# Four store places and five load places in the layer norm of a sparse graph layer

## The chip, the cores and the metric

The kernel runs on one core of a Trainium2 chip. The metric is device time in microseconds (us), the median of several executions. PE is TensorE, DVE is VectorE, ACT is ScalarE, POOL is GpSimd and SP is SyncE, whose queue issues most DMAs. A core's DMAs run on 16 DMA engines.

## The reference

```python
# x: (8192, 512) float32; adj: (8192, 8192) float32, some 0.1% of it above zero, a diagonal among it
h = maximum(layernorm(x), 0)
mask = adj > 0
head = mask / maximum(sqrt(sum(mask * mask, axis=-1)), 1e-12)
inc = adj + head
out = x + (inc @ h) / sum(inc, axis=-1)
```

The layer norm has no weights, and its eps is 1e-5. adj has 256 MB and is read once. x, h and out have 16 MB each.

## The kernel before

**The layer norm (LN).** The 8192 rows are taken in LN = 16 chunks of 512 rows; each of the 128 partitions holds ROWS = 4 rows of 512 values, 8 KB. A chunk is loaded by SP (ln_load, L340), 1 MiB in one DMA. DVE computes its statistics (ln_chunk, L703 to L712), with a root by ACT in between (ln_sqrt, L513). ACT writes relu of the normalised rows into a store place (ln_apply, L520), four instructions, and raises ln_done. SP stores the place to h_scratch in HBM (ln_store, L344), 1 MiB again. h_scratch is what the gathers read later.

**The places.** The first HELD_CHUNKS = 5 chunks are loaded into x_held, where they stay for the residual. The other eleven go round through XBUFS = 3 places of four slots in gathered_rows (G, 22 slots of 512 values). The store places are slots 12 to 19 of the same buffer, two places, taken in turn (hst). ln_apply of chunk c waits on h_stored[c % 2], so for the store of chunk c-2. ln_load of chunk c, from c = 8 on, waits until ln_done is c - XBUFS + 1, so for chunk c-3.

**SP's order.** SP first issues ln_load of chunks 0 to 3. Then for c = 4 to 15 it issues ln_store(c-4), which waits for ln_done of that chunk, and ln_load(c). Then comes chunk 0 of adj's tile 0, and then the last four stores, with adj chunks 1 to 3 of tile 0 between them (load_chunk, L352); then the four chunks of tile 1 with no wait, and from tile 2 on the loads of the scan, each of which waits until DVE and ACT have read the chunk it overwrites (L349, L351).

**The scan.** adj is taken in 64 tiles of 128 rows. adj_tile (A, 128 partitions x 2 x 8192 values) holds two tiles, A[:, t % 2]. A tile is loaded in four chunks of 1 MiB, each 1024 columns of the left and of the right half. For each chunk DVE folds the two halves into one (fold, L720), finds the eight largest words (L742) and their places (L746). ACT counts zeros over the chunks (check, L533). The small operations of the tiles before are placed between these, by an order written out by hand (period). POOL gathers the rows of h that a tile needs by indirect DMA (L454), 8 own slots and 3 spill slots a tile, into gathered_rows. PE sums them with diagonal and spill matrices (L1157, L1165), and brings the spilled entries of a tile together (L1130), for which DVE waits at L863. POOL waits for all of h_stored before its first gather. DVE starts on tile 0 when its part of the layer norm is over.

At the start POOL clears slots 20 and 21 of gathered_rows (L430), which no place of the layer norm uses.

Of the kernel before, what the change touches and what calls it, by code (L numbers as in the profile page):

```python
# [7 lines left out]
def add_graph_layer(nc, x, adj, out):  # L8
# [4 lines left out]
    ACT = mybir.ActivationFunctionType  # L13
    AX = mybir.AxisListType

    N, D = x.shape
# [31 lines left out]
    ROWS = 4  # L48
    LN = N // (P * ROWS)
# [2 lines left out]

    HELD_CHUNKS = 5
    HELD = ROWS * HELD_CHUNKS
    XBUFS = 3

    KB = N // P
    HCH = 8
# [10 lines left out]
    with ctx:  # L69
        def sb(name, shape, dt):  # L70
            return ctx.enter_context(nc.sbuf_tensor(name, shape, dt))

        def sem(name):
            return ctx.enter_context(nc.semaphore(name))

        h = nc.dram_tensor("h_scratch", [N, D], fp32, kind="Internal").ap()
        h_ln = h.rearrange("(c p j) d -> c p j d", p=P, j=ROWS)
        h_blk = h.rearrange("(c k p) d -> c p k d", p=P, k=HCH)

        A = sb("adj_tile", [P, 2, N], fp32)  # L80
        F = sb("folded", [P, 2, CW], fp32)
        G = sb("gathered_rows", [P, 2 * (OWN + EXTRA), D], fp32)
# [91 lines left out]
        def xin(c):  # L174
            if c < HELD_CHUNKS:
                return held[:, ROWS * c:ROWS * (c + 1), :]
            b = (c - HELD_CHUNKS) % XBUFS
            return G[:, ROWS * b:ROWS * (b + 1), :]

        def hst(b):  # L180
            return G[:, ROWS * (XBUFS + b):ROWS * (XBUFS + 1 + b), :]

        def x_of(t):
            return held[:, t] if t < HELD else xres[:, t % 2]
# [10 lines left out]
        def chunk(b, j):  # L195
            return A[:, b, 2 * CW * j:2 * CW * (j + 1)].rearrange("p (h c) -> p h c", h=2)
# [5 lines left out]
        def diag_chunk(t):  # L202
            return t // ROWS * P * ROWS % HALF // CW
# [48 lines left out]
        ln_rstd = sem("ln_rstd")  # L252
        ln_scaled = sem("ln_scaled")
        ln_done = sem("ln_done")
        h_stored = [sem(f"h_stored{b}") for b in range(2)]
        adj_loaded = [[sem(f"adj_loaded{b}{j}") for j in range(CHUNKS)] for b in range(2)]
        x_loaded = [sem(f"x_loaded{b}") for b in range(2)]
        checked = sem("checked")
# [76 lines left out]
        @block.sync  # L335
        def _(sp):
            def ln_load(c):
                if c >= HELD_CHUNKS + XBUFS:
                    sp.wait_ge(ln_done, c - XBUFS + 1)
                sp.dma_start(xin(c), x_ln[c]).then_inc(ln_loaded[c % 8], 16)  # L340

            def ln_store(c):
                sp.wait_ge(ln_done, c + 1)
                sp.dma_start(h_ln[c], hst(c % 2)).then_inc(h_stored[c % 2], 16)  # L344

            def load_chunk(t, j):
                if t >= 2:
                    sp.wait_ge(folded, CHUNKS * (t - 2) + j + 1)
                    sp.wait_ge(checked, 4 * (t - 2) + 2 * (j // 2) + 2)  # L349
                    if j == diag_chunk(t - 2):  # L350
                        sp.wait_ge(diag_read, t - 1)  # L351
                sp.dma_start(chunk(t % 2, j), adj_h[t // ROWS, t % ROWS, :, :, CW * j:CW * (j + 1)]).then_inc(adj_loaded[t % 2][j], 16)  # L352

            def load_x(t):
                if t >= HELD + 2:
                    sp.wait_ge(own_done, t - 1)
                sp.dma_start(xres[:, t % 2], x_t[t // ROWS, t % ROWS]).then_inc(x_loaded[t % 2], 16)

            def store_tile(t):
                sp.wait_ge(out_ready, t + 1)  # L360
                sp.dma_start(out_t[t // ROWS, t % ROWS], osb[:, t % 2]).then_inc(out_stored[t % 2], 16)

            for c in range(4):
                ln_load(c)
            for c in range(4, LN):
                ln_store(c - 4)
                ln_load(c)
            load_chunk(0, 0)
            for c in range(LN - 4, LN):
                ln_store(c)  # L370
                if c < LN - 1:
                    load_chunk(0, c - (LN - 4) + 1)
            for j in range(CHUNKS):
                load_chunk(1, j)
            for t in range(TILES):
                if t + 2 < TILES:
                    load_chunk(t + 2, 0)
                    load_chunk(t + 2, 1)
                if t >= 4:
                    store_tile(t - 4)  # L380
                if t >= HELD:
                    load_x(t)
                if t + 2 < TILES:
                    load_chunk(t + 2, 2)
                    load_chunk(t + 2, 3)
            for t in range(TILES - 4, TILES):
                store_tile(t)
            for b in range(2):
                sp.wait_ge(out_stored[b], 16 * (TILES // 2))

            sp.wait_ge(list_ready, 1)
            n = sp.value_load(badnu[0:1, 0:1], min_val=0, max_val=TILES)
            with sp.If(n > 0):
                with sp.Fori(0, n) as j:
                    row = sp.value_load(badu[0:1, bass.ds(j, 1)], min_val=0, max_val=FIRST_ROW)
                    sp.wait_ge(batch_stored, 16)
                    sp.dma_start(A[:, 0, :], adj[bass.ds(row, P, step=ROWS), :]).then_inc(d_adj, 16)
                    sp.dma_start(xres[:, 0], x[bass.ds(row, P, step=ROWS), :]).then_inc(d_x, 16)
                    for c in range(NCH):
                        if c >= 2:  # L400
                            sp.wait_ge(d_mm, j * KB + (c - 1) * HCH)
                        sp.dma_start(G[:, HCH * (c % 2):HCH * (c % 2 + 1), :], h_blk[c]).then_inc(d_h[c % 2], 16)
                    sp.wait_ge(d_out, j + 1)
                    sp.dma_start(out[bass.ds(row, P, step=ROWS), :], osb[:, 0]).then_inc(d_stored, 16)
                    sp.wait_ge(d_stored, j * 16 + 16)
                    sp.sem_inc(passed, 1)

        @block.gpsimd
        def _(pool):
            steps = [0]  # L410

            def step(ins):
                steps[0] += 1
                ins.then_inc(const_step, 1)
                pool.wait_ge(const_step, steps[0])
# [11 lines left out]
            step(nc.gpsimd.memset(cap[:], 3.0e38))  # L427
            on_diagonal(cap[:], 0, 0.0)
            step(nc.gpsimd.memset(on_diag[:, BATCH:BATCH + 1], 0.0))
            step(nc.gpsimd.memset(G[:, ROWS * (XBUFS + 2):], 0.0))  # L430
            step(nc.gpsimd.memset(ones[:], 1.0))
            step(nc.gpsimd.memset(zero_unit[:], ZERO))
            step(nc.gpsimd.memset(count_eps[:], 1e-24))
# [25 lines left out]
            def gather_own(t):  # L459
                b = t % 2  # L460
                pool.wait_ge(idx_ready, t + 1)
                if t >= 2:
                    pool.wait_ge(own_done, t - 1)
                for s in range(OWN):
                    gather(slot(b, s), idx[:, b, s:s + 1], own_gathered[b][s // CHUNKS])
# [6 lines left out]
                for g in range(EXTRA):  # L472
                    gather(slot(b, OWN + g), spidx[:, b, g:g + 1], spill_gathered[b])

            for b in range(2):
                pool.wait_ge(h_stored[b], 16 * (LN // 2))
            gather_own(0)
            gather_own(1)
            for t in range(2, TILES):
# [30 lines left out]
        def _(act):  # L510
# [3 lines left out]

            def ln_apply(c):
                act.wait_ge(ln_scaled, c + 1)
                if c >= 2:
                    act.wait_ge(h_stored[c % 2], 16 * (c // 2))
                for j in range(ROWS):
                    last = nc.scalar.activation(hst(c % 2)[:, j], xin(c)[:, j], ACT.Relu,  # L520
                                                bias=nb[:, c, j:j + 1], scale=rs[:, c, j:j + 1])
                last.then_inc(ln_done, 1)

# [114 lines left out]
            for c in range(LN):  # L638
                ln_sqrt(c)
                ln_apply(c)  # L640
# [634 lines left out]
```

## Time and profile before

| what | us |
|---|---|
| median of 3 runs | 1341.62 |
| lowest and highest of them | 1336.1, 1348.91 |
| the profiled execution, its own time | 1334.34 |
| span of the profiled execution (first to last instruction) | 1332.6 |

The profile is of one execution. Times in it count from the start of the span. An instruction's busy time is that of its engine; a DMA issue on SP is short, and its transfer runs on the DMA engines afterwards. The DMA share is the mean busy share of the 16 DMA engines, and GB/s is what they moved; a share near 1 with few GB/s means packets that took long.

### The profile page before, as it was taken

The page shows a single profiled execution, that of the slowest core. Times are in us where ns is not written, and L with a number is a line of the kernel's source. Part 1 is how long each engine was busy: PE and PEld are TensorE (multiplying, and loading weights), DVE is VectorE, ACT ScalarE, POOL GpSimd, SP SyncE. Part 2 cuts the span into 40 slices and gives each one's busy share as a digit, 9 for nine tenths or more (in the row PEclk, how much of TensorE's full clock was granted, in tenths as well). Part 3 has the DMA queues.
Part 4 walks back from the last instruction along what each step waited for, and adds up shares of the span by engine and source line. Part 5 has one row for each costly group of instructions (what it writes and reads, how often), then busy time and mean ns, then how long its engine had stood idle before and what let it go on. Part 6 is the DMA issues. An engine that isn't in the chain of part 4 may idle for free.

```text
span 1332.6 us, 14627 instructions
## 1 busy us (share of the span) xinstructions
PE 940.4 (71%) x2670; PEld 457.0 (34%) x2670; DVE 1168.8 (88%) x2845; ACT 978.6 (73%) x1905; POOL 777.0 (58%) x746
## 2 busy tenths in 40 slices
PE   0000887867887887787887888887788878788634
PEld 0000343333443443333443333443343433343312
DVE  5549999889989999898999899999799899898253
ACT  5447886878887887887888787778788788787321
POOL 1002567556676667576667675666666666677413
PEclk9999999899998999998899988989999989999677
DMA  8999999999999999999999999999999999996321
GB/s 346 336 353 406 396 375 376 340 377 356 380 390 345 377 393 388 377 388 373 385 392 389 372 391 375 390 377 376 383 397 391 388 388 388 383 382 227 108 84 42
DMA packets 147390, 469.14 MB, mean 352 GB/s; under 512 B 24752, under 2 KB 24752, under 8 KB 143149
## 3 DMA queue, kind: packets, MB, share of 16 engines
q1 hardware_dynamic: 89792, 330.33, 64.5%
q0 software_dynamic: 57504, 137.85, 28.7%
q8 instruction: 24, 0.39, 0.1%
q14 instruction: 70, 0.57, 0.1%
HBM read 488.64 MB, written 33.82 MB: 392 GB/s over the span
## 4 chain that ended last, share of the span: by engine, by line
DVE 63%; issue 18%; DMA 6%; another core or an unknown queue 5%; ACT 5%; POOL 1%; PE 1%; DVEq 0%; SPq 0%; ACTq 0%; POOLq 0%
DVE cand_word L742 21%; DVE folded L720 21%; DVE cand_index L746 8%; DMA h_scratch<-gathered_rows 5%; ACT gathered_rows L520 2%; ACT junk L533 1%; DVE diagonal_alone L727 1%; DVE entry L878 1%; DVE folded L736 1%; DVE weights_and_payload L841 1%; DMA adj_tile<-in_adj_dram,bad_row_number 1%; DVE entry_sign L784 1%; DVE inc L829 1%; ACT diag L592 1%
## 5 line engine op out<-in xcount | busy, mean ns | idle before, releaser
L454 POOL DMA_INDIRECT gathered_rows<-h_scratch,slot_column x520 | 559.6, 1076 | 310.9 <-issue 159.0
L1157 PE MATMUL acc<-gathered_rows,diag 128*128 128x512 f32 x1040 | 494.6, 620 | 90.3 <-DMA gathered_rows<-h_scratch,slot_column 74.7
L533 ACT ACTIVATE junk<-adj_tile,zero_unit 128x2048 bf16<-128x2048 f32 x256 | 509.9, 2000 | 4.9 <-DMA adj_tile<-in_adj_dram 4.9
L454 POOL DMA_INDIRECT gathered_rows<-h_scratch,spill_column x195 | 208.5, 1069 | 227.3 <-ACT spill_column L575 163.5
L1157 PEld LDWEIGHTS acc<-gathered_rows,diag 128*128 128x128 f32 x1040 | 197.3, 197 | 339.0 <-issue 338.8
L742 DVE MAX8 cand_word<-folded 128x8 f32<-128x1024 f32 x256 | 312.8, 1222 | 0.5 <-issue 0.3
L746 DVE FIND_INDEX8 cand_index<-cand_word,folded 128x8 uint32<-128x1024 f32 x256 | 312.2, 1219 | 0.0
L720 DVE SCALAR_TENSOR_TENSOR folded<-adj_tile 128x1024 f32<-128x1024 f32 x256 | 310.9, 1215 | 0.0
L1165 PE MATMUL acc<-gathered_rows,spill_matrix 128*128 128x512 f32 x390 | 220.6, 711 | 90.8 <-DMA gathered_rows<-h_scratch,spill_column 74.1
L592 ACT ACTIVATE diag<-ident,weights_and_payload 128x128 f32<-128x128 f32 x584 | 177.3, 387 | 32.7 <-issue 17.6
L1165 PEld LDWEIGHTS acc<-gathered_rows,spill_matrix 128*128 128x128 f32 x390 | 81.7, 223 | 181.2 <-issue 181.2
L609 ACT ACTIVATE out_tile<-acc 128x512 f32<-128x512 f32 x65 | 38.5, 593 | 133.4 <-remote 63.7
L1112 PE MATMUL poff<-spill_rank,lanes_before 128*128 128x1 f32 x128 | 18.2, 212 | 120.0 <-DVE spill_rank L791 119.8
L1151 PE MATMUL acc<-own_row,diag 128*128 128x512 f32 x128 | 71.7, 644 | 42.9 <-ACT own_row L602 26.3
L1112 PEld LDWEIGHTS poff<-spill_rank,lanes_before 128*128 128x128 f32 x128 | 24.3, 192 | 150.5 <-issue 149.0
L863 DVE TENSOR_TENSOR own_entry<-pbrought,place_plus_half 128x72 f32<-128x72 f32 (+1 forms) x65 | 14.8, 228 | 65.1 <-remote 58.5
L1130 PEld LDWEIGHTS pbrought<-weights_and_payload,owner 128*128 128x128 f32 x390 | 54.8, 195 | 36.8 <-issue 36.8
L520 ACT ACTIVATE gathered_rows<-gathered_rows,ln_bias,ln_rstd 128x512 f32<-128x512 f32 x44 | 32.2, 802 | 36.7 <-DMA h_scratch<-gathered_rows 36.7
L1136 PE MATMUL pturned<-ident,owner 128*128 128x128 f32 x390 | 58.4, 287 | 0.0
L1130 PE MATMUL pbrought<-weights_and_payload,owner 128*128 128x72 f32 (+1 forms) x390 | 53.2, 274 | 5.1 <-issue 3.7
L583 ACT ACTIVATE spill_matrix<-pturned,entry 128x128 f32<-128x128 f32 x195 | 56.8, 366 | 0.0
L1151 PEld LDWEIGHTS acc<-own_row,diag 128*128 128x128 f32 x128 | 23.7, 199 | 80.3 <-issue 55.4
(152 smaller groups left out, 860.2 us busy)
## 6 DMA issues: line engine op xcount, KB each, us to landing
adj_tile<-in_adj_dram SPq DMA_DIRECT2D x256, 1024.0 KB
h_scratch<-gathered_rows SPq DMA_DIRECT2D x16, 1024.0 KB, 8.9
out_dram<-out_tile SPq DMA_DIRECT2D x64, 256.0 KB
gathered_rows<-in_x_dram SPq DMA_DIRECT2D x11, 1024.0 KB, 7.3
x_residual<-in_x_dram SPq DMA_DIRECT2D x44, 256.0 KB
gathered_rows<-h_scratch,slot_column POOLq DMA_INDIRECT x520
x_held<-in_x_dram SPq DMA_DIRECT2D x5, 1024.0 KB, 8.1
gathered_rows<-h_scratch,spill_column POOLq DMA_INDIRECT x195
```

Source lines behind the costliest of these rows:

```text
L454: nc.gpsimd.indirect_dma_start(out=into, out_offset=None, in_=h[:, :], in_offset=bass.IndirectOffsetOnAxis(ap=column, axis=0), bounds_chec ...
L520: last = nc.scalar.activation(hst(c % 2)[:, j], xin(c)[:, j], ACT.Relu, bias=nb[:, c, j:j + 1], scale=rs[:, c, j:j + 1])
L533: nc.scalar.activation(junk[:, n % 2].rearrange("p (j c) -> p j c", j=2), both[:, :, half], ACT.Relu, bias=zero_unit[:], scale=-UP, accum_ ...
L592: last = nc.scalar.activation(diag[:, t % 2, s], ident[:], ACT.Copy, scale=wpay[:, t % 2, s:s + 1])
L720: nc.vector.scalar_tensor_tensor(out=F[:, j % 2], in0=a[:, 1], scalar=UP, in1=a[:, 0], op0=ALU.mult, op1=ALU.add).then_inc(folded, 1)
L742: nc.vector.max(out=cv[:, t % 2, 8 * j:8 * j + 8], in_=F[:, j % 2]).then_inc(vals_found, 1)
L746: nc.vector.max_index(out=ci[:, t % 2, 8 * j:8 * j + 8], in_max=cv[:, t % 2, 8 * j:8 * j + 8], in_values=F[:, j % 2]).then_inc(idx_found, 1)
L1130: last = nc.tensor.matmul(pbrought[:, 3 * n * g:3 * n * (g + 1)], owner[:, g * P:(g + 1) * P], wpay[:, t % 2, 1 + OWN:1 + OWN + 3 * n], st ...
L1136: last = nc.tensor.matmul(pturned[:, g * P:(g + 1) * P], owner[:, g * P:(g + 1) * P], ident[:], start=True, stop=True)
L1151: nc.tensor.matmul(acc[t % 3][:], diag[:, t % 2, 0], again[:], start=False, stop=False)
L1157: last = nc.tensor.matmul(acc[t % 3][:], diag[:, t % 2, 1 + s], slot(t % 2, s), start=False, stop=False)
L1165: last = nc.tensor.matmul(acc[t % 3][:], W[:, t % 2, g], slot(t % 2, OWN + g), start=False, stop=(g == EXTRA - 1))
```

## The change

XBUFS goes from 3 to 5, so loaded chunks from the sixth on go round through five places, slots 0 to 19 of gathered_rows. The store places leave gathered_rows: there are four, in the half of adj_tile that holds tile 1 (A[:, 1]), a quarter of it each. h_stored has four semaphores instead of two. Because the stores read what tile 1's loads overwrite, SP now waits for all stores before it issues the first chunk of tile 1.

```diff
-    XBUFS = 3
+    XBUFS = 5
...
         def hst(b):
-            return G[:, ROWS * (XBUFS + b):ROWS * (XBUFS + 1 + b), :]
+            return A[:, 1, ROWS * D * b:ROWS * D * (b + 1)].rearrange("p (j d) -> p j d", j=ROWS)
...
-        h_stored = [sem(f"h_stored{b}") for b in range(2)]
+        h_stored = [sem(f"h_stored{b}") for b in range(4)]
...
             def ln_store(c):
                 sp.wait_ge(ln_done, c + 1)
-                sp.dma_start(h_ln[c], hst(c % 2)).then_inc(h_stored[c % 2], 16)
+                sp.dma_start(h_ln[c], hst(c % 4)).then_inc(h_stored[c % 4], 16)
...
                 if c < LN - 1:
                     load_chunk(0, c - (LN - 4) + 1)
+            for b in range(4):
+                sp.wait_ge(h_stored[b], 16 * (LN // 4))
             for j in range(CHUNKS):
                 load_chunk(1, j)
...
-            step(nc.gpsimd.memset(G[:, ROWS * (XBUFS + 2):], 0.0))
+            step(nc.gpsimd.memset(G[:, ROWS * XBUFS:], 0.0))
...
-            for b in range(2):
-                pool.wait_ge(h_stored[b], 16 * (LN // 2))
+            for b in range(4):
+                pool.wait_ge(h_stored[b], 16 * (LN // 4))
...
             def ln_apply(c):
                 act.wait_ge(ln_scaled, c + 1)
-                if c >= 2:
-                    act.wait_ge(h_stored[c % 2], 16 * (c // 2))
+                if c >= 4:
+                    act.wait_ge(h_stored[c % 4], 16 * (c // 4))
                 for j in range(ROWS):
-                    last = nc.scalar.activation(hst(c % 2)[:, j], xin(c)[:, j], ACT.Relu,
+                    last = nc.scalar.activation(hst(c % 4)[:, j], xin(c)[:, j], ACT.Relu,
                                                 bias=nb[:, c, j:j + 1], scale=rs[:, c, j:j + 1])
```

## Rows read from the trace of the kernel before

**Rows 1.** The page: busy time by engine, and two of its costliest groups.
```profile
PE 940.4 (71%) x2670; PEld 457.0 (34%) x2670; DVE 1168.8 (88%) x2845; ACT 978.6 (73%) x1905; POOL 777.0 (58%) x746
...
L1157 PE MATMUL acc<-gathered_rows,diag 128*128 128x512 f32 x1040 | 494.6, 620 | 90.3 <-DMA gathered_rows<-h_scratch,slot_column 74.7
...
L720 DVE SCALAR_TENSOR_TENSOR folded<-adj_tile 128x1024 f32<-128x1024 f32 x256 | 310.9, 1215 | 0.0
```

**Rows 2.** Table of stretches: from:to, us; engines' busy time (count); PE clock, DMA share, GB/s.
```profile
0.00:38.00 38.00, 0.00 (x0) 0.00 (x0) 22.07 (x75) 21.09 (x34) 5.87 (x28) 1.00 0.89 354
...
21.00:38.00 17.00, 0.00 (x0) 0.00 (x0) 9.62 (x33) 9.45 (x17) 0.00 (x0) 1.00 1.00 420
38.00:43.00 5.00, 0.00 (x0) 0.00 (x0) 3.18 (x11) 3.09 (x7) 0.00 (x0) 1.00 0.92 220
43.00:51.00 8.00, 0.00 (x0) 0.00 (x0) 3.65 (x14) 3.07 (x6) 0.00 (x0) 1.00 0.96 402
...
76.00:82.00 6.00, 0.00 (x0) 0.00 (x0) 3.38 (x12) 3.02 (x5) 0.00 (x0) 1.00 0.81 255
82.00:90.00 8.00, 0.00 (x0) 0.00 (x0) 3.89 (x13) 3.02 (x5) 0.00 (x0) 1.00 0.97 338
...
38.00:98.10 60.10, 0.00 (x0) 0.00 (x0) 29.36 (x101) 27.32 (x47) 0.00 (x0) 1.00 0.93 337
98.10:113.70 15.60, 0.00 (x0) 0.00 (x0) 15.26 (x21) 10.98 (x12) 0.00 (x0) 1.00 1.02 406
...
0.00:113.67 113.67, 0.00 (x0) 0.00 (x0) 66.65 (x195) 59.39 (x91) 5.87 (x28) 1.00 0.93 352
```

**Rows 3.** Waits from 0 to 130 us: us in total, times, longest.
```profile
ACT gathered_rows L520 <- DMA h_scratch<-gathered_rows: 43.2, 14, 6.8
...
DVE ln_stats L703 <- DMA gathered_rows<-in_x_dram: 6.1, 5, 1.7
```

**Rows 4.** The tile h_scratch from 0 to 125 us: issue to landing of its DMAs.
```profile
DMA to landing us min/median/max: 4.8/8.9/12.3
```

**Rows 5.** Timeline of the first 20 us: start, duration, engine, line, operation.
```profile
0.80 2.04 SPq L340 DMA_DIRECT2D x_held<-in_x_dram  x4
...
5.72 2.47 DVE L703 BATCH_NORM_STATS2 ln_stats<-x_held 128x6 f32<-128x512 f32 x4 [5.72 <-DMA x_held<-in_x_dram]
...
14.00 2.48 DVE L703 BATCH_NORM_STATS2 ln_stats<-x_held 128x6 f32<-128x512 f32 x4
...
17.51 2.47 DVE L703 BATCH_NORM_STATS2 ln_stats<-x_held 128x6 f32<-128x512 f32 x4
```

**Rows 6.** Timeline around 38 us: chunk 8's load, chunk 5's store, chunk 8's statistics.
```profile
38.05 0.33 SPq L340 DMA_DIRECT2D gathered_rows<-in_x_dram  x1
...
38.43 0.43 SPq L344 DMA_DIRECT2D h_scratch<-gathered_rows  x1
...
45.02 2.47 DVE L703 BATCH_NORM_STATS2 ln_stats<-gathered_rows 128x6 f32<-128x512 f32 x4 [1.56 <-DMA gathered_rows<-in_x_dram]
```

**Rows 7.** Timeline of the hand-over from the layer norm to the scan.
```profile
94.74 2.93 ACT L520 ACTIVATE gathered_rows<-gathered_rows,ln_bias,ln_rstd 128x512 f32<-128x512 f32 x4 [6.75 <-DMA h_scratch<-gathered_rows]
...
98.12 1.23 DVE L720 SCALAR_TENSOR_TENSOR folded<-adj_tile 128x1024 f32<-128x1024 f32 x1
...
102.66 0.33 SPq L344 DMA_DIRECT2D h_scratch<-gathered_rows  x1
103.03 58.43 SPq L352 DMA_DIRECT2D adj_tile<-in_adj_dram  x20
...
113.67 1.21 DVE L720 SCALAR_TENSOR_TENSOR folded<-adj_tile 128x1024 f32<-128x1024 f32 x1
```

**Rows 8.** Two later stretches, and DVE's longest waits from 98 to 1270 us.
```profile
100.00:165.00 65.00, 28.26 (x76) 13.95 (x77) 64.58 (x135) 50.38 (x82) 26.49 (x25) 0.97 1.02 401
...
230.00:295.00 65.00, 49.69 (x148) 24.46 (x146) 55.64 (x133) 49.95 (x100) 38.96 (x39) 0.94 0.97 364
...
DVE own_entry L863 <- remote: 58.5, 15, 7.8
```

## The prediction, made before the change was run

> **What bounds the kernel now.** The page comes first. VectorE (DVE) is busy 88% of the span, more than any other engine, its fold of a chunk (L720) had no idle time before it in 256 executions, and PE's product with gathered rows (L1157) waited 74.7 us for gathers [rows 1]. That is a mean over stages. The change touches only the layer norm (about 0 to 103 us) and the hand-over to the scan of adj, so I read those by themselves.
>
> The table of stretches shows two kinds of time in the layer norm [rows 2]. From 21 to 38 us the DMA engines move 420 GB/s at a share of 1.00. After that slow and fast stretches alternate: 220 GB/s in 38 to 43 us, 402 in 43 to 51, and so on to 255 in 76 to 82 (four slow stretches, at 38, 51, 63 and 76 us). From 38 to 98.1 us the mean is 337 GB/s, while DVE works 29.4 us of 60.1 and ScalarE (ACT) 27.3.
>
> The waits say who is late: ACT's layer-norm pass (L520) waited 43.2 us in 14 waits for a store to h_scratch to land, DVE only 6.1 us in 5 for a load [rows 3]. A store takes 8.9 us in the median from issue to landing, 12.3 at most [rows 4]. So the loop is: chunk c is normalised, its store is issued, it lands 8.9 us later, and only then may chunk c+2 be written into the same place, which takes 2.93 us plus 0.5 us of root, reciprocal and bias. (8.9 + 3.4) / 2 = 6.2 us a chunk. The trace has the L520 pass over chunk 14 begin at 94.74, after 6.75 us of waiting [rows 7]. The work itself could go faster: DVE's statistics of chunks 2 and 3 start 3.51 us apart (14.00 and 17.51) [rows 5].
>
> **The change, part by part.** *Four store places instead of two.* Chunk c now waits for the store of chunk c-4: (8.9 + 3.4) / 4 = 3.1 us a chunk, less than the 3.5 us of the compute chain. Even a store of 12.3 us [rows 4] gives only 3.9. This wait ceases to decide. What is late next is the transfer itself: each chunk is a 1 MiB load and a 1 MiB store, 2.10 MB, or 5.2 us at 406 GB/s and 5.0 us at 420. The layer norm becomes bound by DMA bandwidth.
>
> *Five load places instead of three.* The load of c now waits for chunk c-5, but SP issues the store of c-4 just ahead of it, which waits for chunk c-4. So SP runs four chunks ahead, not five; before it was three. Four chunks ahead is 4 x 5.2 = 20.7 us from one load to the time its chunk must be done, less about 6.6 us from landing to normalised; 14 us of transfers stay queued, over 5 MB. The queue does not run dry. Before, load and store issued at 38.05 and 38.43 met a nearly empty queue and the load was only read at 45.02, 7 us on [rows 6].
>
> *What rate.* This is the largest unknown. Upper end: 420 GB/s, loads and stores mixed with a queue that held several transfers (21 to 38 us). Lower end: 337, the mean of 38 to 98.1 us, if the slow stretches belong to the mixture and not to the nearly empty queue. For the empty queue: the first slow stretch follows one, and the fast stretch behind it has the next pair of transfers issued on top. Against: 82 to 90 us ran at 338 GB/s [rows 2], with the last load of x, two chunks of adj and stores queued, by SP's order. I take 406, the rate of 98.1 to 113.7 us, in which a full queue of adj loads and the last stores runs.
>
> *The sum to the hand-over.* The first 38 us stay as they are: 354 x 38 = 13.45 MB moved, and the last 17 of them at full rate already. Only the four first loads are issued up front, as before. In SP's order the last store is the 36th transfer of 1.049 MB (16 loads, 16 stores, 4 chunks of tile 0), so 37.75 MB. At 406 GB/s its last byte goes at 38 + (37.75 - 13.45) / 0.406 = 97.9 us (95.9 at 420, 110.1 at 337).
>
> *The new wait of SP.* Before, tile 1's first chunk was issued at 103.03, right behind the last store at 102.66 [rows 7]. Now SP waits until all 16 stores have landed, since the four places lie in tile 1's buffer. Behind that wait stands everything that SP issues from tile 1 on, first the four loads of tile 1; DVE's fold of chunk (1,0) and ACT's check of (1,0) and (1,1) wait for them. I add about 0.8 us until the last store is confirmed (an estimate between 0 and 2.3 us: the shortest store took 4.8 us [rows 4], of which 1.05 MB at 420 GB/s are 2.5, and the rest lies at both its ends), and 4.9 us for a load into an empty queue, from the issue at 0.80 to DVE's start at 5.72 [rows 5]. Chunk (1,0) is folded at 97.9 + 5.7 = 103.6 us instead of 113.67 [rows 7]: 10.1 us earlier (12.1 at 420, 2.1 later at 337). The chunks behind it come every 2.6 us, and DVE needs 3.7 to 3.9, so the gap is paid once.
>
> *Tile 0.* Load 15 is transfer 28: 77.2 us, with about 1 us to land; DVE's last layer-norm operations end some 3.4 us later, so the first fold comes near 82 instead of 98.12 us. Sixteen us, but they are not kept: the rest of tile 0's chunks alternate with stores, 5.2 us apart, so DVE waits between folds, and chunk (0,3) comes at 38 + (36.7 - 13.45) / 0.406 + 1 = 96.3 us. Its 3.7 us of work end before the 103.6 of chunk (1,0). No engine's work grows: the same 64 passes of L520, 16 loads and 16 stores. POOL waits on four semaphores for one moment, long before its first gather needs anything. SP's semaphore waits cost nothing where they are already met.
>
> *What the rest keeps.* From 100 to 165 us DVE is busy 64.58 of 65 us and DMA has a share of 1.02; from 230 to 295 DVE has 55.64 of 65 [rows 8]. Its largest wait is L863, 58.5 us in 15 waits, for what PE brings over. PE in turn waits for gathers [rows 1], which share the DMA engines. If DVE's position sets the rest, all 10.1 us stay. If DMA's position does, less: after the change 38.8 MB (36 transfers and one chunk) are moved by 103.6 us, before by 38.8 / 0.352 = 110.2 us [rows 2], 6.6 us. For the first tiles DVE is nearer the bound, over the whole run both; I take 8.5 us.
>
> In the profiled execution (1334.34 us, span 1332.6) that makes 1325.8. It lies 7.3 us under the median of the three runs; on the median, 1341.6 - 8.5 = 1333.1 us.
>
> **The rivals.**
> *A: the mixture of loads and stores is what is slow; the new wait then decides.* Place: SP's wait for all stores. At 337 GB/s the last store's byte goes at 110.1 us, chunk (1,0) is folded at 115.8, 2.1 us late, and 38.8 MB are moved then instead of at 110.2, 5.6 us late. Price: 2 to 6 us slower, 1346 us in the middle. It decides below 24.3 / (113.67 - 5.7 - 38) = 347 GB/s. For it: 338 GB/s in 82 to 90 us, with transfers queued, and the DMA share of 0.93 over the whole slow part. Against: 420 GB/s for 17 us on the same mixture.
>
> *B: a ceiling between the two.* A rate near 358 GB/s would put the last byte at 105.9 and the fold at 111.6, 2 us gained by DVE and 1.4 us lost by the DMA position (111.6 against 110.2): 1341 us, no change. The rows speak against it as a ceiling with 420, 402 and 406 GB/s. The Trainium skill, "DMA: Bandwidth & Descriptors", section "Where 436 GB/s comes from", says that for transfers between HBM and SBUF the HBM side, about 358 GB/s for a core, binds. By that rule this change would bring nothing. The trace does not agree: its own rows reach 420 GB/s.
>
> *C: the hand-over is early, and the gain is given back.* The rest of the run waits on gathers and PE in a loop of its own, and starts with 3 to 4 adj chunks less loaded ahead than before. If that lead carried the first tiles, stalls at L863 come sooner: a gain of 0 to 4 us, 1340 us. For it: DMA shares of 0.97 to 1.03 to the end. Against: DVE never waited for an adj load [rows 1].
>
> *D: more than forecast.* 420 GB/s or more (12.1 us at the fold) and an emptier queue for the first gathers: 12 to 18 us, 1327 us.
>
> That the change doesn't do what it says is true of one place of five (SP never gets that far ahead); it is priced above.
>
> **How the numbers follow.** Forecast (gain of 5 to 12 us) 0.55; A 0.15; B 0.05; C 0.12; D 0.13. A measurement here can tell about 1% (13.4 us) from no change. Faster by more than that needs under 1328.2 us: most of D and the edge of the forecast, 0.17. Slower by more needs over 1355, which even A reaches only with later stalls added: 0.03. The rest, 0.80, lies within 1%. The range reaches from D's 1322 to A's 1346 us; the three runs of before are themselves 13 us apart.
>
> **What would show each step.** L520's waits for h_scratch fall from 43.2 us to under 8; DVE's waits for loads (L703) grow past 15 us; the stretch from 38 us on shows 400 GB/s or more without slow stretches of 220 to 260; stores take longer to land (over 11 us); the first fold is near 82 us; a DMA gap of 2 to 4 us stands before tile 1; chunk (1,0) is folded near 104 us; POOL's first gather is 9 to 10 us earlier. The prediction is wrong if the rate stays under 350 GB/s, if the fold of (1,0) is not before 110 us, or if it is and the end does not follow.

## The result, and the profile after

The change measured 1327.07 us (median of 20 executions) against 1341.98 us for the kernel before (20): a ratio of 0.9887, 95% interval 0.986 to 0.9914. A second measurement of the same pair, on another chip (e12 below), gave 0.9956, 0.9918 to 0.9995. Each ratio leaves out the executions that are over 1.5% above the fastest of their kernel: five of the change's 20 (one of them, at 1392.47 us, ran with a granted clock of 0.70 instead of 0.93), by the same bound four of the 20 before, and, in the second measurement, seven of the 17 of the kernel before but none of the change's 12. The medians of all executions are 14.9 us apart in the first measurement and 10.5 us in the second. Both intervals exclude 1, but they do not overlap each other, so the size is known only roughly: 15.2 us by the first and 5.9 by the second. Weighted by their widths the two ratios make 0.991, or 12 us, which is a compromise and not a measurement. The forecast was 1333.1 us in a range of 1322 to 1346, a ratio of 0.9937.

The profiled execution took 1328.75 us. The table of stretches of the changed kernel answers to [rows 2], in the same columns:

```profile
38.00:43.00 5.00, 0.00 (x0) 0.00 (x0) 3.37 (x13) 3.45 (x6) 0.00 (x0) 1.00 1.02 429
...
76.00:82.00 6.00, 0.00 (x0) 0.00 (x0) 5.50 (x16) 4.22 (x8) 0.00 (x0) 1.00 1.01 418
82.00:90.00 8.00, 0.00 (x0) 0.00 (x0) 6.62 (x8) 4.71 (x5) 0.00 (x0) 1.00 1.02 428
90.00:98.10 8.10, 0.00 (x0) 0.00 (x0) 6.68 (x8) 3.89 (x3) 0.00 (x0) 1.00 0.69 265
98.10:113.70 15.60, 2.12 (x5) 1.13 (x5) 12.13 (x27) 8.93 (x13) 2.29 (x2) 1.00 1.01 404
38.00:98.10 60.10, 0.00 (x0) 0.00 (x0) 43.70 (x117) 36.86 (x53) 0.00 (x0) 1.00 0.97 404
```

The slow stretches are gone. From 38 to 90 us the DMA engines move 418 to 429 GB/s, where they had alternated between some 220 to 260 and some 400. Then comes a gap, 265 GB/s in 90 to 98.1 us: SP waits for the last store. By the us it looks like this:

```profile
94.00:95.00 1.00, 0.00 (x0) 0.00 (x0) 0.87 (x1) 0.79 (x1) 0.00 (x0) 1.00 0.82 344
95.00:96.00 1.00, 0.00 (x0) 0.00 (x0) 0.97 (x2) 1.00 (x1) 0.00 (x0) 1.00 0.06 25
96.00:97.00 1.00, 0.00 (x0) 0.00 (x0) 0.96 (x3) 1.00 (x3) 0.00 (x0) 1.00 0.00 0
```

The waits from 0 to 130 us answer to [rows 3], and the landing of the stores to [rows 4]:

```profile
DVE ln_stats L705 <- DMA gathered_rows<-in_x_dram: 14.5, 11, 1.6
...
DVE folded L722 <- DMA adj_tile<-in_adj_dram: 6.0, 4, 3.6
```

```profile
DMA to landing us min/median/max: 4.9/10.5/13.9
```

ACT's 43.2 us of waiting for stores have no row any more. In its place DVE waits for loads, 14.5 us in 11 waits: the layer norm is bound by what the DMA engines can move. A store takes longer than before (10.5 us), and no engine waits for it until the last one. The hand-over, answering to [rows 7], from the timeline of the changed kernel:

```profile
79.61 1.23 DVE L722 SCALAR_TENSOR_TENSOR folded<-adj_tile 128x1024 f32<-128x1024 f32 x1
...
82.65 0.33 SPq L344 DMA_DIRECT2D h_scratch<-adj_tile  x1
...
94.13 1.22 DVE L722 SCALAR_TENSOR_TENSOR folded<-adj_tile 128x1024 f32<-128x1024 f32 x1 [1.13 <-DMA adj_tile<-in_adj_dram]
...
96.64 18.82 SPq L352 DMA_DIRECT2D adj_tile<-in_adj_dram  x12
...
101.50 1.23 DVE L722 SCALAR_TENSOR_TENSOR folded<-adj_tile 128x1024 f32<-128x1024 f32 x1 [3.56 <-DMA adj_tile<-in_adj_dram]
```

The first fold comes 18.5 us earlier than before, the last chunk of tile 0 is folded at 94.13, SP is released at 96.64 and chunk (1,0), the first of tile 1, is folded 4.86 us later, at 101.50 us, 12.2 us before the 113.67 of [rows 7]. DVE's longest wait of the later run stands as in [rows 8]:

```profile
DVE own_entry L865 <- remote: 62.4, 14, 7.8
```

The lead of 12.2 us is still there six tiles later. Chunk (7,0) is folded at these times, before and after the change, 12.3 us apart:

```profile
213.77 1.22 DVE L720 SCALAR_TENSOR_TENSOR folded<-adj_tile 128x1024 f32<-128x1024 f32 x1
```
```profile
201.48 1.22 DVE L722 SCALAR_TENSOR_TENSOR folded<-adj_tile 128x1024 f32<-128x1024 f32 x1
```

After that the stalls at L863 (L865 after the change), up to 7.8 us each, fall differently in each execution. At chunk (32,0) these two are only 1.0 us apart (660.52 and 659.53 us).

### The profile page after: what moved, and what is told of

Its sections match the earlier page's. It is cut to its first block, busy times and chain, and to the rows that moved or that the text cites. A ratio compares the mean times of both kernels' runs of the same rounds, so it can differ in the third digit from the quotient of the medians.

```text
span 1326.7 us, 14628 instructions
## 1 busy us (share of the span) xinstructions
PE 941.3 (71%) x2670; PEld 457.6 (34%) x2670; DVE 1169.6 (88%) x2845; ACT 978.6 (74%) x1905; POOL 785.1 (59%) x746
## 4 chain that ended last, share of the span: by engine, by line
DVE 65%; issue 17%; DMA 5%; another core or an unknown queue 5%; ACT 3%; PE 3%; POOL 1%; DVEq 0%; SPq 0%; POOLq 0%; ACTq 0%
DVE cand_word L744 21%; DVE folded L722 21%; DVE cand_index L748 8%; DMA gathered_rows<-in_x_dram 3%; ACT adj_tile L522 2%; PE acc L1159 1%; DVE diagonal_alone L729 1%; DVE entry L880 1%; DVE folded L738 1%; DMA h_scratch<-adj_tile 1%; DVE weights_and_payload L843 1%; DMA adj_tile<-in_adj_dram,bad_row_number 1%; DVE entry_sign L786 1%; DVE inc L831 1%
## 5 line engine op out<-in xcount | busy, mean ns | idle before, releaser
L535 ACT ACTIVATE junk<-adj_tile,zero_unit 128x2048 bf16<-128x2048 f32 x256 | 510.0, 2000 | 14.5 <-DMA adj_tile<-in_adj_dram 14.5
L456 POOL DMA_INDIRECT gathered_rows<-h_scratch,spill_column x195 | 215.9, 1107 | 226.2 <-ACT spill_column L577 169.3
L1114 PE MATMUL poff<-spill_rank,lanes_before 128*128 128x1 f32 x128 | 18.6, 215 | 110.2 <-DVE spill_rank L793 110.0
L865 DVE TENSOR_TENSOR own_entry<-pbrought,place_plus_half 128x72 f32<-128x72 f32 (+1 forms) x65 | 14.7, 226 | 67.6 <-remote 62.4
L535 ACT ACTIVATION_READ_ACCUMULATOR junk<-adj_tile,zero_unit 128x1 f32 x256 | 50.9, 199 | 0.0
L1138 PEld LDWEIGHTS pturned<-ident,owner 128*128 128x128 f32 x390 | 50.1, 196 | 0.0
## 6 DMA issues: line engine op xcount, KB each, us to landing
h_scratch<-adj_tile SPq DMA_DIRECT2D x16, 1024.0 KB, 10.5
```

The lines of the kernel that those rows point to most:

```text
L456: nc.gpsimd.indirect_dma_start(out=into, out_offset=None, in_=h[:, :], in_offset=bass.IndirectOffsetOnAxis(ap=column, axis=0), bounds_chec ...
L535: nc.scalar.activation(junk[:, n % 2].rearrange("p (j c) -> p j c", j=2), both[:, :, half], ACT.Relu, bias=zero_unit[:], scale=-UP, accum_ ...
L1138: last = nc.tensor.matmul(pturned[:, g * P:(g + 1) * P], owner[:, g * P:(g + 1) * P], ident[:], start=True, stop=True)
```

## The experiments

Twelve runs were made in three groups (e1 to e4, e7 to e10, e11 to e14), each group on one chip beside the kernel before. The load gate is the wait that ties the load of chunk c to an earlier chunk: with a gate of three it waits until chunk c-3 is normalised. "Fold" is when DVE folds chunk (1,0) in the profiled execution. The kernel before was profiled for the sections above and again as e11, but not on the chip of e7 to e10. The gain is (1 - ratio) times the median of the kernel before in that group (1335.02, 1287.09 and 1333.61 us; 1341.98 in the first measurement).

| kernel | mean GB/s, 38 to 98.1 us | fold, us | ratio (95% interval) | gain, us |
|---|---|---|---|---|
| the change, first measurement | 404 | 101.50 | 0.9887 (0.986 to 0.9914) | 15.2 |
| e1, load gate of three | 402 | 102.40 | 0.9906 (0.9876 to 0.9935) | 12.5 |
| e2, two store places | 403 | 102.67 | 0.993 (0.9894 to 0.9966) | 9.3 |
| e3, wait per place | 425 | 99.37 | 0.991 (0.9874 to 0.9946) | 12.0 |
| e4, before with the wait | 328 | 117.38 | 1.0033 (0.9997 to 1.0069) | -4.4 |
| e7, both gates as before | 360 | 110.78 | 1.0015 (0.9997 to 1.0032) | -1.9 |
| e8, loads in tile 1's buffer, two stores | 426 | 103.81 | 0.9912 (0.9897 to 0.9927) | 11.3 |
| e9, the same, four stores | 424 | 99.50 | 0.9891 (0.9874 to 0.9907) | 14.0 |
| e10, the same, six loads up front | 424 | 96.62 | 0.988 (0.9863 to 0.9897) | 15.4 |
| e11, before again | 339 | 112.60 | | |
| e12, the change again | 404 | 101.67 | 0.9956 (0.9918 to 0.9995) | 5.9 |
| e13, change, six loads up front | 398 | 99.12 | 0.9886 (0.9826 to 0.9945) | 15.2 |
| e14, e13 with the wait per place | 423 | 96.87 | 0.9876 (0.9812 to 0.9941) | 16.5 |

**e1: the load gate of three.**
```diff
-                if c >= HELD_CHUNKS + XBUFS:
-                    sp.wait_ge(ln_done, c - XBUFS + 1)
+                if c >= HELD_CHUNKS + 3:
+                    sp.wait_ge(ln_done, c - 3 + 1)
```


> The changed kernel, but the load of chunk c waits for chunk c-3 again, as with three load places (four store places, tile 1 waits for all stores). Theory (the store places did it; the load places are not what counts): three chunks ahead are 3 x 4.9 = 14.8 us less 6.6 us of computing, so 8 us or 3.5 MB stay queued, the DMA rate stays 425 GB/s from 21 us on, chunk (1,0) is folded at 101 to 103 us, ratio 0.987 to 0.991. Rival (both parts are needed): slow stretches of 220 to 260 GB/s return between 38 and 82 us, the fold comes at 106 to 112 us, ratio 0.993 to 1.0.

As the theory had it. The five load places are not needed for the rate when there are four store places. From the table of stretches of e1:

```profile
38.00:43.00 5.00, 0.00 (x0) 0.00 (x0) 3.41 (x12) 3.06 (x6) 0.00 (x0) 1.00 1.00 423
...
76.00:82.00 6.00, 0.00 (x0) 0.00 (x0) 5.05 (x16) 4.17 (x7) 0.00 (x0) 1.00 1.03 421
```

**e2: two store places.**
```diff
-                if c >= 4:
-                    act.wait_ge(h_stored[c % 4], 16 * (c // 4))
+                if c >= 2:
+                    act.wait_ge(h_stored[c % 2], 16 * (c // 2))
...
-                    last = nc.scalar.activation(hst(c % 4)[:, j], xin(c)[:, j], ACT.Relu,
+                    last = nc.scalar.activation(hst(c % 2)[:, j], xin(c)[:, j], ACT.Relu,
```
(and ln_store, the semaphores and both waits for all stores to match.)

> The changed kernel with two store places instead of four (five load places, tile 1 waits for all stores). Theory (the wait of ACT for the store of chunk c-2 bounded the layer norm): ACT's waits for h_scratch are back at 35 us or more, L520 runs once in 6 us, the mean rate from 38 to 98 us is 340 GB/s, the fold of chunk (1,0) comes at 112 to 117 us because the wait for all stores is now added, ratio 0.998 to 1.004. Rival (one chunk more of loads ahead is enough to keep the DMA queue filled): no slow stretches, the fold before 106 us, ratio under 0.992.

My theory fell here. ACT waits for stores again, in 14 waits as before, yet no stretch from 38 to 90 us is under 421 GB/s, and DVE's waits for loads into gathered_rows have no row. From the waits, the landing of the stores and the stretches of e2:

```profile
ACT adj_tile L522 <- DMA h_scratch<-adj_tile: 30.7, 14, 4.4
```
```profile
DMA to landing us min/median/max: 4.9/6.9/10.3
```
```profile
38.00:43.00 5.00, 0.00 (x0) 0.00 (x0) 3.25 (x12) 3.02 (x5) 0.00 (x0) 1.00 1.02 429
```

A store lands after 6.9 us, so two places allow (6.9 + 3.4) / 2 = 5.2 us a chunk, close to the 4.9 us that 2.10 MB need at 426 GB/s. The 8.9 us of [rows 4] were not a property of a store. The same two places give 6.9 us where the slow stretches are missing, so the 8.9 us were the effect of these as much as the cause. With four chunks of loads ahead the two places are enough. The fold is at 102.67 us, 10 us earlier than the theory said.

**e3: SP waits per place.** Place j lies exactly under chunk j of tile 1.
```diff
-            for b in range(4):
-                sp.wait_ge(h_stored[b], 16 * (LN // 4))
             for j in range(CHUNKS):
+                sp.wait_ge(h_stored[j], 16 * (LN // 4))
                 load_chunk(1, j)
```


> The changed kernel, but SP waits ahead of chunk (1,j) only for the last store of place j instead of for all stores. Theory (the wait for all stores costs a gap in the DMA at the hand-over, 95.0 to 98.9 us, and nothing else): chunk (1,0) is issued near 83 us, queued behind the last store, no gap, folded at 98.0 to 98.5 us instead of 101.5, ratio to the kernel before 0.984 to 0.988, so 3 to 4 us better than the change. Rival (the later stages take it back): the fold is as early, the time stays at the ratio of the change, 0.989 or more.

The gap is gone, from the stretches and the timeline of e3:

```profile
90.00:98.10 8.10, 0.00 (x0) 0.00 (x0) 6.84 (x8) 3.63 (x3) 0.00 (x0) 1.00 1.01 420
```
```profile
83.63 29.70 SPq L352 DMA_DIRECT2D adj_tile<-in_adj_dram  x12
...
99.37 1.23 DVE L721 SCALAR_TENSOR_TENSOR folded<-adj_tile 128x1024 f32<-128x1024 f32 x1 [1.17 <-DMA adj_tile<-in_adj_dram]
```

Tile 1's first load is issued at 83.63 instead of 96.64 us. The fold comes 2 to 3 us earlier, a us less than expected, because tile 0 itself is paced by its chunks, 5 us apart. In time that doesn't show: 12.0 us of gain beside 12.5 for e1 on the same chip, each good to 4 or 5 us. The rival is neither shown nor excluded by this run.

**e4: the kernel before with only the new wait.**
```diff
+            for b in range(2):
+                sp.wait_ge(h_stored[b], 16 * (LN // 2))
             for j in range(CHUNKS):
                 load_chunk(1, j)
```


> The kernel before with only the new wait added: SP waits until all stores have landed ahead of tile 1's first load. The last store landed at 102.66 + 7.5 = 110.2 us before, so chunk (1,0) is issued there and folded 4.9 us later, at 115.1 instead of 113.67. Theory that DVE's position sets the rest: 1 to 2 us slower, ratio 1.000 to 1.002. Theory that the DMA position sets the rest: 38.8 MB are moved at 115.1 instead of 110.2 us, 5 us slower, ratio 1.003 to 1.005. Rival of the prediction in which the wait decides: 5 us and more.

From the timeline of e4:

```profile
112.43 6.92 SPq L352 DMA_DIRECT2D adj_tile<-in_adj_dram  x8
117.38 1.23 DVE L722 SCALAR_TENSOR_TENSOR folded<-adj_tile 128x1024 f32<-128x1024 f32 x1 [2.08 <-DMA adj_tile<-in_adj_dram]
```

DVE waited 2.08 us for the chunk; the other 1.6 us of 117.38 against 113.67 were lost in this execution's layer norm already (its first fold is at 99.67, not 98.12). The price of the wait alone is about 2 us at the fold. In time the run is 4.4 us slower, with an interval from -0.4 to 9, so a loss is likely and not shown. This is rival A with the rate of the layer norm unchanged, and it is why the change had to win more than that.

**e7: both gates as before, in the new buffer.** The edits of e1 and e2 together.

> The changed kernel with both limits as before: two store places, and the load of chunk c waits for chunk c-3. What is left of the change is where the store places lie (tile 1's buffer instead of gathered_rows) and the wait for all stores. The two runs that put back one limit each kept 425 GB/s. Theory Q (either limit loosened keeps the queue filled, both tight let it run dry): slow stretches of 220 to 290 GB/s return between 38 and 90 us, mean 325 to 345 from 38 to 98 us, chunk (1,0) folded at 114 to 118 us, ratio 0.999 to 1.006, like the kernel before with the wait added. Theory P (the place of the buffer matters, not how many): no slow stretches, 400 GB/s and more, fold at 101 to 107 us, ratio 0.988 to 0.994.

This separates the causes. From the stretches and the waits of e7:

```profile
38.00:43.00 5.00, 0.00 (x0) 0.00 (x0) 3.05 (x11) 3.02 (x5) 0.00 (x0) 1.00 0.94 249
...
51.00:56.00 5.00, 0.00 (x0) 0.00 (x0) 2.15 (x10) 3.02 (x5) 0.00 (x0) 1.00 0.86 270
...
38.00:98.10 60.10, 0.00 (x0) 0.00 (x0) 32.28 (x106) 29.29 (x48) 0.00 (x0) 1.00 0.98 360
```
```profile
ACT adj_tile L522 <- DMA h_scratch<-adj_tile: 39.5, 14, 5.1
```

The slow stretches are back, with stores out of tile 1's buffer. So it is theory Q: with either limit loosened the rate stays at 402 GB/s or more, gap included, and with both tight it falls every second chunk. Where the places lie is not it. The mean of 360 and the fold at 110.78 are better than I had said, while the ratio is 1.0015. The four profiles with both limits tight have means of 328, 337, 339 and 360 GB/s, so slow stretches vary from one execution to the next, and one fold need not be that of the others. Whether the kernel before folds chunk (1,0) at 110 or at 113 us on this chip is not known.

**e8 and e9: loads in tile 1's buffer, stores in gathered_rows.** Then tile 1 need not wait for stores.
```diff
-    XBUFS = 3
+    XBUFS = 4
...
         def xin(c):
...
-            return G[:, ROWS * b:ROWS * (b + 1), :]
+            return A[:, 1, ROWS * D * b:ROWS * D * (b + 1)].rearrange("p (j d) -> p j d", j=ROWS)
...
         def hst(b):
-            return G[:, ROWS * (XBUFS + b):ROWS * (XBUFS + 1 + b), :]
+            return G[:, ROWS * b:ROWS * (b + 1), :]
...
             pool.sem_inc(consts_set, 1)
+            step(nc.gpsimd.memset(G[:, ROWS * 4:2 * (OWN + EXTRA) - 2], 0.0))
```
(e9 has four store places, with four semaphores and ACT's, SP's and POOL's waits and indices to match, which are not shown; e8 keeps two, and clears from slot ROWS * 2 on. The clear of slots 20 and 21 stays where it was.)

> The other way round: four load places in tile 1's buffer, two store places in gathered_rows, no wait for all stores ahead of tile 1 (its loads overwrite only chunks that are normalised by then). POOL clears the unused slots behind its other constants. The load of chunk c waits for chunk c-4. Theory Q (depth): 420 GB/s or more from 21 us on, as with two store places in the other buffer, ACT's waits for h_scratch 25 to 35 us, no gap at the hand-over, chunk (1,0) folded at 98 to 101 us. Theory P (place, in the sense that stores out of gathered_rows are slow): slow stretches as before, mean under 350 GB/s, fold at 110 us or later.

> Four load places in tile 1's buffer, four store places in gathered_rows, no wait for all stores. It keeps what the change gains in the layer norm and loses the gap in front of tile 1. Expected by the DMA arithmetic: 425 GB/s from 21 us without a gap to 113 us, chunk (1,0) folded at 98.0 to 99.5 us as with the wait per place, ratio to the kernel before 0.984 to 0.991. If the later stages take the last 3 us back, the time is that of the change.

Both run at 424 GB/s or more without a gap. e9 folds chunk (1,0) at 99.50 us and gains 14.0 us, on a chip where the interval is only 2 us wide to each side. e8 folds at 103.81, later than said, for a reason at its very start, from its timeline:

```profile
8.49 5.26 DVE L709 TENSOR_SCALAR ln_var_eps<-ln_mean_var 128x4 f32<-128x4 f32 x1
8.51 5.22 POOL L452 MEMSET gathered_rows<- 128x6144 f32 x1 [0.15 <-POOL first_row_plus_one L418]
```

The operation on 128x4 values, 0.17 us in the median of its 16, lasted until POOL's clearing had ended. That put off the first store from 13.55 to 17.39 us. DVE's first fold of tile 0 then came at 88.26 us, against 84.64 in e2, which also has two store places, and from there e8's folds up to chunk (1,0) stand 3.7 to 4.4 us apart with no wait for a load.

**e10: e9 with six loads up front.**
```diff
-            for c in range(4):
+            AHEAD = 6
+            for c in range(AHEAD):
                 ln_load(c)
-            for c in range(4, LN):
-                ln_store(c - 4)
+            for c in range(AHEAD, LN):
+                ln_store(c - AHEAD)
                 ln_load(c)
             load_chunk(0, 0)
-            for c in range(LN - 4, LN):
+            for c in range(LN - AHEAD, LN):
                 ln_store(c)
-                if c < LN - 1:
-                    load_chunk(0, c - (LN - 4) + 1)
+                if c - (LN - AHEAD) + 1 < CHUNKS:
+                    load_chunk(0, c - (LN - AHEAD) + 1)
```


> The kernel with four load and four store places and no wait, and with six loads issued up front instead of four, so that the DMA queue does not run empty at 12.5 us. Theory (an empty queue, and the slow restart after it, cost 1.5 us of idle and 7 us at 300 GB/s): 425 GB/s from 3 us on with no stretch below 390 up to 95 us, chunk (1,0) folded 3 to 4 us earlier than with four loads up front, 94 to 96 us, ratio 0.981 to 0.988. Rival (the slow restart belongs to the first stores, not to the empty queue): a stretch of 300 GB/s appears when the stores begin, and the fold is at 97 us or later.

Half and half. The idle time at 12.5 us is gone and the fold comes 2.9 us earlier. But a slow start of the stores stands although loads are queued ahead of and behind them, from e10's table by the us:

```profile
14.00:15.00 1.00, 0.00 (x0) 0.00 (x0) 0.85 (x3) 0.56 (x2) 0.00 (x0) 1.00 1.03 434
...
16.00:17.00 1.00, 0.00 (x0) 0.00 (x0) 1.00 (x5) 1.00 (x3) 0.00 (x0) 1.00 1.17 254
17.00:18.00 1.00, 0.00 (x0) 0.00 (x0) 0.66 (x7) 0.61 (x2) 0.00 (x0) 1.00 0.83 188
```

The first store was issued at 13.98. So an empty queue is not the only thing that makes packets slow. In all profiles the stretch after the first stores is slow (279 to 375 GB/s from 14 to 21 us; in e8, whose first store is late, the stretch moves with it). The runs agree with this reading: stores that start after a pause run slowly for a few us, and a queue that always holds stores avoids the pause. No run tests it for the slow stretches after 38 us, and why stores start slowly no run here shows.

**e11 to e14: the two kernels again, and six loads up front in the change** (e13 has e10's edit on the changed kernel, e14 that and e3's).

> The kernel before once more, for a second profile of its layer norm on another chip or at another time. If the slow stretches belong to the kernel, they stand again between 38 and 90 us (220 to 290 GB/s in the slow ones, mean of 38 to 98 us 325 to 365), with the fold of chunk (1,0) at 108 to 116 us; if they were an accident of one execution, the mean is over 400.

> The changed kernel once more, for its ratio beside the other designs on one chip. The hand-over is at 101 to 102.5 us. If DVE's position at the hand-over is kept whole, the ratio is 0.990 to 0.992 where the kernel before folds chunk (1,0) at 113.7, and each us of an earlier fold in the two runs below is a us of time. If the later stages keep half, the ratio is 0.994 to 0.996.

> The changed kernel with six loads up front instead of four; the wait for all stores stays. The DMA queue is filled from 3 us on except for the slow start of the stores near 15 to 18 us; last store's byte near 92 us, chunk (1,0) folded at 97.5 to 99 us, 3 us before the change. Time 1.5 to 3 us under the change; if the later stages take it back, none.

> The changed kernel with six loads up front and the wait per place. Both gaps are gone: DMA at 420 GB/s from 21 us to 113 us without a gap, chunk (1,0) folded at 94 to 97 us. Time 3 to 7 us under the change (ratio to the kernel before 0.985 to 0.989), the best of all if the hand-over is kept; equal to the change if it isn't.

e11's stretches show that the slow stretches belong to the kernel:

```profile
51.00:56.00 5.00, 0.00 (x0) 0.00 (x0) 3.18 (x11) 3.11 (x6) 0.00 (x0) 1.00 0.59 156
...
38.00:98.10 60.10, 0.00 (x0) 0.00 (x0) 30.10 (x101) 27.20 (x45) 0.00 (x0) 1.00 0.93 339
```

e12's layer norm is that of the first profile to 0.2 us, and yet its ratio says 5.9 us, not 15.2. The two profiles fold chunk (1,0) at the same time, so the difference lies behind the layer norm, in the kernel before or in the spread: executions of the change are 19 us apart there (1311.43 to 1330.67), and the medians of all executions differ by 10.5 us. No run separates these. e13 and e14 fold at 99.12 and 96.87 us and have the best medians of their group (1319.24 and 1318.53 against 1323.07 for the change), but their intervals overlap with the change's.

## Why the prediction was right, and which steps were not

**The place and the course: right.** The layer norm went from waiting on stores to waiting on loads (DVE 14.5 us; I had said past 15), the first fold came at 79.6 (82), chunk (0,3) was folded at 94.1 (96.3), and the wait for all stores cost a gap ahead of chunk (1,0), at 101.5 (103.6). From SP's release to the fold it took 4.86 us, the 4.9 us of the first load in [rows 5]. POOL's first gather began 12.2 us earlier (123.20 and 111.05 us; I had said 9 to 10). Stores landed after 10.5 us (I had said over 11), so the queue stayed filled, though with less than the 14 us of transfers that I had worked out. Rival A (the mixture is slow) and rival B (a ceiling near 358 GB/s) are excluded by 418 to 429 GB/s on the same mixture.

**The rate: too low, and partly made up by the last store.** I took 406 GB/s, the rate behind the hand-over; measured were 418 to 429 in every stretch from 38 to 90 us. By the 406 the last store's data should have gone at 97.9 us; but for some 25 KB they had gone at 95.0 (the table by the us above). From there SP was released after 1.6 us, at 96.64, where I had added 0.8. Of 2.9 us won 0.8 are lost again, and 2.1 us of error are left at the fold. My sum at 420 GB/s, 12.1 us at the fold where 12.2 were measured, fits only because the two errors nearly cancel in it. The 338 GB/s of 82 to 90 us before, which had held me back, did not return. The Trainium skill, "DMA: Bandwidth & Descriptors", section "Bandwidth", has 341 GB/s for a single 1 MB load and 425 for one of 16 MB, measured on loads issued from GpSimd. The trace reaches the second of these, 418 to 429 GB/s, with a filled SP queue of 1 MiB loads and stores.

**What decides: half wrong.** "This wait ceases to decide" was true of the change, but I had made the two store places the bound by themselves, from a landing time that the slow stretches had made long. e2 keeps them and gets the full rate; e1 keeps the three-chunk gate and gets it too; only e7, with both, is slow. The load places were not a side matter, as my loop of 6.2 us a chunk had them: for the rate, either part of the change would have done.

**What the rest keeps: too little.** I took 8.5 of 10.1 us, halfway between DVE's position and the DMA's. The result shows the lead of 12.2 us still at 12.3 us in chunk (7,0). On the chip of e7 to e10, where stalls at L863 are few, it can be followed further. Chunk (32,0) is folded at 633.73 us in e7, 626.68 in e8, 622.43 in e9 and 619.56 in e10; the first and the last of these are

```profile
633.73 1.22 DVE L722 SCALAR_TENSOR_TENSOR folded<-adj_tile 128x1024 f32<-128x1024 f32 x1
```
```profile
619.56 1.22 DVE L722 SCALAR_TENSOR_TENSOR folded<-adj_tile 128x1024 f32<-128x1024 f32 x1
```

Over e7 that is a lead of 7.1, 11.3 and 14.2 us, and at chunk (1,0) it was 7.0, 11.3 and 14.2. The medians of the three lie 10.9, 13.4 and 15.5 us under that of e7. So DVE's position is kept whole over half of the scan, and at the end no less than the lead is left.

Over all runs the same holds as far as the intervals allow. Against the mean fold of the two profiles of the kernel before, 113.1 us, the folds lie 11.6 and 11.5 us earlier (the change's two profiles), 10.7 (e1), 10.4 (e2), 13.7 (e3), 9.3 (e8), 13.6 (e9), 16.5 (e10), 14.0 (e13), 16.2 (e14) and 4.3 later (e4). The gains are 15.2 and 5.9 (the change's two measurements), 12.5, 9.3, 12.0, 11.3, 14.0, 15.4, 15.2, 16.5 and -4.4. Lead and gain differ by 2 us or less except for the change's own two measurements, where the gain is 3.6 us over and 5.6 under the lead, and for e7 (2.3 earlier, gain -1.9). The gains are good to 2 us each way for e7 to e10, where the 113.1 us come from other chips, to 4 or 5 for most others, and to 8 or 9 for e13 and e14. Rival C, which takes the lead back in the first tiles, is excluded by chunk (7,0). By the DMA position of my own sum 8.7 us would have been kept (110.2 less 101.5); the first measurement, 11.5 to 18.8 us, excludes that, the second, 0.7 to 10.9, doesn't.

**The size.** Of the 3.5 us between my 8.5 and the weighted 12, 2.1 are the earlier fold and the rest is what the later stages were thought to take. The wide range held both measurements (1327.07 and 1323.07 us). The narrower forecast, a gain of 5 to 12 us, holds the second (5.9) and not the first (15.2), which lies in rival D's 12 to 18 us, at a chance of 0.13. D was right in its rate. Its other reason, emptier queues for the first gathers, is not seen: from (1,0) to (7,0) the lead grew by 0.1 us. By the forecast's own bound of 1%, the first measurement is a gain a little over it and the weighted one a little under.

**A better version.** e10 and e14 fold chunk (1,0) 5 us before the change and have the lowest ratios (0.988 and 0.9876). On the chip of e8 to e10 the order of e8, e9 and e10 is that of their folds (1276.78, 1274.24, 1272.2 us). That e10 or e14 beats the change itself is likely from the fold, and is not measured beyond the intervals.

## What to carry to other kernels

Where loads and stores run through a few places, look at the DMA rate by stretches of some us before blaming the store that somebody waits for: a mean of 337 GB/s was an alternation of 220 to 262 and 384 to 413, and one load place more (e8) or two store places more (e1) brought 425. A staging buffer can lie in memory that is idle then. Let each of its first users wait for its own place only (e3), or put there what is consumed early, the loads (e9), rather than what must be written back, the stores: both removed the gap and brought the fold 2 us forward, though e3's time did not show it. Where DVE is the bound behind a prologue, as here, look whether the lead at the hand-over still stands some tiles on; here it stood whole.

## What the runs showed that was not expected

The first stores of e10 ran slowly, 188 to 254 GB/s for some 2 us, with loads queued on both sides, so the queue's depth in bytes is not all that counts.

A POOL memset of 128x6144 values went with a DVE tensor_scalar on 128x4 values of 5.26 us instead of 0.17 (e8). With the smaller memset of e9, 128x2048 values in 1.80 us, it took 1.85 us. The Trainium skill, "SBUF — State Buffer", section "Who interferes with whom", says that DVE's two-port modes and POOL share one pair of ports, which is held for a whole instruction. The trace agrees, with DVE's end 0.02 us after POOL's in e8; that this instruction ran in a two-port mode no view shows.

The group of e7 to e10 ran, in the profiles, at a granted clock of 0.951 to 0.961 instead of 0.93, and the kernel before took 1287 us there instead of 1335. DVE's waits at L863 for what PE brings over, 58.5 us in [rows 8], are down to some 10 us in that group, and it waits for adj instead. From the waits of e9 from 98 to 1270 us:

```profile
DVE folded L721 <- DMA adj_tile<-in_adj_dram: 14.8, 15, 2.1
...
DVE own_entry L864 <- PE pbrought L1131: 9.1, 4, 3.2
```

DVE itself is busy as long (1168.8 us before, 1168.7 in e7), so the 47 us between their spans (1332.6 and 1285.5) are idle time of DVE. The lower clock and the longer waits go together in all profiles here, but the clock changes only with the chip, so that the one causes the other is not shown. Nor is it shown that these stalls are what makes executions scatter; the spread is 31 us for the 17 of the kernel before in the group of e12 and 8 us for the 17 in the group of e7.
